# Second layer's self-attention: 32-row score groups, column-grouped values, an unrolled loop

## What is computed

```python
cq = _layernorm(x @ W_dq, q_ln_g, q_ln_b)          # 256 -> 64
Q = cq @ W_uq                                      # 64 -> 256
ckv = _layernorm(x @ W_dkv, kv_ln_g, kv_ln_b)
KV = ckv @ W_ukv
K, V = (KV[..., :D], KV[..., D:])
q, k, v = (t.reshape(B, S, N_HEADS, DH) for t in (Q, K, V))
scores = jnp.einsum('bqhd,bkhd->bhqk', q, k) / math.sqrt(float(DH))
scores = scores * jnp.tril(jnp.ones((S, S)))
scores = jnp.where(scores == 0, -jnp.inf, scores)  # also where a product is exactly 0
attn = jax.nn.softmax(scores, axis=-1)
out = jnp.einsum('bhqk,bkhd->bqhd', attn, v).reshape(B, S, D)
return out @ W_o.T
```

## Time and profile before

| | us |
|---|---|
| median of 3 runs (lowest to highest) | 4347.18 (4345.33 to 4351.53) |
| the profiled execution, its own time | 4351.41 |
| its span, first to last instruction | 4349.6 |
| its mean granted TensorE clock | 0.885 of full speed |

### The profile page before, as it was taken

One profiled execution on the slowest core, in us unless ns is written; L12 is line 12 of the kernel. 1 busy time (PEld: TensorE's weight loads), 2 busy tenths in 40 slices (PEclk: granted clock), 3 DMA queues, 4 the chain that ended last, 5 costly groups with the idle time before them and its releaser, 6 DMA issues. The chain is left out here.

```text
span 4349.6 us, 51903 instructions
## 1 busy us (share of the span) xinstructions
PE 3389.6 (78%) x16452; PEld 2208.8 (51%) x16453; DVE 2264.0 (52%) x5392; ACT 1485.2 (34%) x4021; POOL 864.8 (20%) x829
## 2 busy tenths in 40 slices
PE   6585994747989889856697688897888868876994
PEld 3553672325767667633374365344563345654663
DVE  6545553436666656457863466315642365743223
ACT  3212661213544545333102244213432124531331
POOL 2103012041010010110151545004520030030113
PEclk9776997868999999978798899898999889987997
DMA  1000001010000000000000000000000000013112
GB/s 55 1 1 11 1 1 63 5 46 1 1 2 2 1 2 1 19 30 10 0 1 13 26 1 1 27 0 26 1 6 22 15 11 7 1 50 142 33 34 69
DMA packets 34663, 80.29 MB, mean 18 GB/s; under 512 B 8433, under 2 KB 23554, under 8 KB 30306
## 3 DMA queue, kind: packets, MB, share of 16 engines
q1 hardware_dynamic: 28594, 63.03, 4.0%
q0 software_dynamic: 4368, 11.93, 1.0%
q10 hardware_dynamic: 1440, 2.12, 0.1%
HBM read 63.04 MB, written 14.02 MB: 18 GB/s over the span
## 5 line engine op out<-in xcount | busy, mean ns | idle before, releaser
L2159 PE MATMUL psum<-KT,Q_heads 128*128 x768 | 298.8, 500 | 23.0 <-DVE Q_heads L2199 23.0
L2171 PE MATMUL psum<-probsT,V_heads 128*128 128x128 f32 x2304 | 304.0, 278 | 0.0
L2220 DVE TENSOR_SCALAR zero_marks<-psum 128x128 f32<-128x128 f32 (+7 forms) x256 | 193.8, 757 | 199.7 <-PE psum L2162 199.6
L2171 PEld LDWEIGHTS psum<-probsT,V_heads 128*128 128x128 f32 x2304 | 284.3, 195 | 0.0
L2242 ACT ACTIVATE scores<-scores,max 128x128 f32<-128x128 f32 (+7 forms) x256 | 198.1, 774 | 158.4 <-DVE max L2224 157.2
L2254 ACT ACTIVATE probsT<-psum 128x128 f32<-128x128 f32 (+7 forms) x256 | 166.5, 650 | 214.1 <-PE psum L2186 214.1
L213 POOL TENSOR_SCALAR Xtok<-Xtok,ln_stats 128x256 f32<-128x256 f32 x144 | 174.2, 1217 | 295.2 <-DVE ln_stats L192 295.2
L2186 PE MATMUL psum<-ident,scores 128*128 128x128 f32 x1152 | 181.2, 284 | 62.9 <-ACT scores L2242 61.1
L2222 DVE CUSTOM_DVE_ANT_0 scores<-psum,zero_marks 128x128 f32<-128x128 f32 (+7 forms) x256 | 194.1, 758 | 30.6 <-issue 1.9
L2145 POOL TENSOR_TENSOR V_heads<-V,head_cols 128x1024 f32<-128x1024 f32 x32 | 81.8, 2590 | 594.5 <-PE psum L2171 527.6
L2186 PEld LDWEIGHTS psum<-ident,scores 128*128 128x128 f32 x1152 | 124.2, 142 | 140.7 <-ACT scores L2242 138.5
(11 more groups left out here) (606 smaller groups left out, 7360.5 us busy)
## 6 DMA issues: line engine op xcount, KB each, us to landing
W<-in_L3f_W SPq DMA_DIRECT2D x16, 1024.0 KB, 20.9
L3f_y_rows<-y SPq DMA_DIRECT2D x39, 128.0 KB, 1.7
L0f_rows<-Xtok SPq DMA_DIRECT2D x2, 2048.0 KB, 8.0
W<-in_L0f_W SPq DMA_DIRECT2D x3, 1152.0 KB
Wqkv<-in_L2f_Wqkv SPq DMA_DIRECT2D x2, 1536.0 KB, 8.5
W<-in_L2f_W SPq DMA_DIRECT2D x2, 1536.0 KB
XT<-in_xT SPq DMA_DIRECT2D x1, 2048.0 KB, 7.9
Xtok<-in_xtok SPq DMA_DIRECT2D x1, 2048.0 KB, 13.1
```

What stands on the lines that cost most here:

```text
L2159: pe.matmul(sc(i)[:, o:e], Qh[:, q % 2, h, :], KT[:, bass.ds(u * S + o, e - o)], start=True, stop=(e < n), skip_group_check=True)
L2171: ins = pe.matmul(ob(q)[:, 0:P], Vh[:, kt, h, :], PT[:, i % 2, kt * P:(kt + 1) * P], start=(h == 0 and kt == 0), stop=(h == HPC - 1 and kt ...
L2220: dve.tensor_scalar(zero[:, 0:n], sc(i)[:, 0:n], 0.0, NEG, ALU.is_equal, ALU.mult)
```

## The change

- The zeros that separate heads move. An array row group of 32 holds two heads. The projections write two copies of the queries, `Q[:, par]`, each with the heads of the other parity zeroed and with -1/4 already multiplied in (`sign`). A score product then uses only the 32 rows of its pair of heads. `Q_heads` and its DVE work are gone; since the scores are negated, the kernel takes a minimum, with `scale=-1.0` in the exponential, and the scaling of the maximum (L2224) is gone.
- For blocks 5 to 8 the keys from 512 on are projected into the partitions turned by 64, and `Qt` holds the queries turned likewise, so the two halves of one step's keys lie in two different row groups and in two PSUM banks.
- The values: V is kept in two copies by parity, and a product has 32 stationary columns, that pair's, and writes 32 output partitions. Heads are taken in the order 0, 2, 4, 6, 1, 3, 5, 7, and the values of four steps (a quad, four different column groups) are issued together after every fourth `turn`. `V_heads` and its POOL work are gone; POOL spreads the reciprocals instead of DVE.
- The loop is written out, 256 steps in one sequence. The score buffer in SBUF has 3 slots (2 before), probsT 6 (2 before). PE's order is turn(i), score(i+2), and after each fourth step the quad. ACT's order is exponential(i+1), then copy(i), the other way round than before.
- Projections are one phase (`L1_attn_projections`) with 4 more query jobs of 512 columns and wider weights; a small phase makes `masked` and `sign`. The output is written to the other activation buffer, the keys to the present one.

The diff, cut to its core:

```diff
+HALF_TURN = P // 2
+HEAD_ORDER = (0, 2, 4, 6, 1, 3, 5, 7)
+QUAD = 4
+def L1_attn_projections(nc, K, cT, uq, ukv, sign, Q, Qt, KT, V):
+    for c in range(DC):
+        for j in range(NB):
+            cols = slice(j * BLK, (j + 1) * BLK)
+            jobs.append(("Q", uq[:, c * P:(c + 1) * P], c_block(j), [Q[:, par, c, cols] for par in range(2)]))
+            if j % 2 == 1:
+                jobs.append(("Q", uq[:, D + c * P:D + (c + 1) * P], c_block(j), [Qt[:, par, c, j // 2, :] for par in range(2)]))
+            k0 = 2 * D if j % 2 == 1 else 0
+            jobs.append(("K", ukv[:, k0 + c * P:k0 + (c + 1) * P], c_block(j), [KT[:, c, cols]]))
+    for t in range(NT):
+        jobs.append(("V", cT[:, t * P:(t + 1) * P], ukv[:, D:2 * D], [V[:, par, :, t, :] for par in range(2)]))
...
+            ROT, SLOTS = 3, 6
...
                 @block.tensor
+                    def score(i):
+                        g, par, n = h // 2, h % 2, keys_of(i)
+                        here = slice(32 * g, 32 * g + 32)
+                        there = slice(32 * ((g + 2) % 4), 32 * ((g + 2) % 4) + 32)
+                        if i >= 2:
+                            pe.wait_ge(s["min_done"], i - 1)
+                        first = min(n, BLK)
+                        pe.matmul(sc(i)[:, 0:first], Q[here, par, c, t0:t0 + P], KT[here, c, b * S:b * S + first],
+                                  start=True, stop=(n > BLK), skip_group_check=True)
+                        if n > BLK:
+                            pe.matmul(sc(i)[:, BLK:n], Qt[there, par, c, b, (q - TPB) * P:(q - TPB + 1) * P], KT[there, c, b * S + BLK:b * S + n],
+                                      start=True, stop=False, skip_group_check=True)
+                        pe.matmul(sc(i)[:, n - P:n], K.identb[:], masked[:], start=False, stop=True, skip_group_check=True).then_inc(s["scored"], 1)
+                    def turn(i):
+                        pe.wait_ge(s["exp_done"], i + 1)
+                        if i >= 1:
+                            pe.wait_ge(s["pt_out"], i)
+                        for kt in range(keys_of(i) // P):
+                            ins = pe.transpose(turned[:, kt * P:(kt + 1) * P], Sc[:, i % ROT, kt * P:(kt + 1) * P], K.ident[:])
+                    def values(quad):
+                        pe.wait_ge(s["pt_out"], i0 + QUAD)
+                        for kt in range(q + 1):
+                            for i in range(i0, i0 + QUAD):
+                                g = slice(32 * (h // 2), 32 * (h // 2) + 32)
+                                ins = pe.matmul(ob(u)[g, 0:P], V[:, h % 2, c, b * QT_ + kt, g], PT[:, i % SLOTS, kt * P:(kt + 1) * P],
+                                                start=(first and kt == 0), stop=(last and kt == q), skip_group_check=True)
+                    for i in range(N):
+                        turn(i)
+                        if i + 2 < N:
+                            score(i + 2)
+                        if i % QUAD == 0 and i > 0:
+                            values(i // QUAD - 1)
...
                 @block.vector
+                        dve.wait_ge(s["scored"], i + 1)
+                        if i >= ROT:
+                            dve.wait_ge(s["turned"], i - ROT + 1)
+                        if i >= 2:
+                            dve.wait_ge(s["min_done"], i - 1)
+                        dve.tensor_scalar(zero[:, i % 2, 0:n], sc(i)[:, 0:n], 0.0, -NEG, ALU.is_equal, ALU.mult)
+                        dve.drain()
+                        dve.tensor_tensor_reduce(Sc[:, i % ROT, 0:n], sc(i)[:, 0:n], zero[:, i % 2, 0:n], 1.0, -NEG, ALU.add, ALU.min,
+                                                 low[:, i % ROT:i % ROT + 1]).then_inc(s["min_done"], 1)
...
                 @block.scalar
+                        if i + 1 < N:
+                            exp(i + 1)
+                        act.wait_ge(s["turned"], i + 1)
+                        if i >= SLOTS:
+                            act.wait_ge(s["pv_done"], (i - SLOTS) // QUAD + 1)
+                        act.activation(PT[:, i % SLOTS, 0:n], turned[:, 0:n], ACT.Copy).then_inc(s["pt_out"], 1)
```

More of the change, by code:

```diff
@@ L2092, in L1_attn @@
                 arrive(nc, K)
[L2093 to L2104, removed]
+                with phase(nc, K.sems, "step") as (block, s):
@@ L2120, in L1_attn @@
             Rx, RT = (sbuf(inside, nc, n, [P, 2, P]) for n in ("recip_spread", "recipT"))
[L2121 to L2125 removed]
+            units = [(c, b, q) for c in range(DC) for b in range(B) for q in range(QT_)]
+            steps = [(u, h) for u in range(len(units)) for h in HEAD_ORDER]
+            N, U = len(steps), len(units)
+            keys_of = lambda i: (units[steps[i][0]][2] + 1) * P
@@ L2126, in L1_attn @@
+            names = "scored min_done exp_done turned pt_out pv_done recip_done r_spread r_turned rt_out out"
             with phase(nc, K.sems, names) as (block, s):
                 sc = lambda i: K.psum[:, 2 * (i % 2):2 * (i % 2) + 2, :].rearrange("p b k -> p (b k)")
[L2128 to L2138, removed]
+                turned = K.psum[:, 4:6, :].rearrange("p b k -> p (b k)")
+                ob = lambda u: K.bank[6 + u % 2]
@@ L2148, in _ @@
                 @block.tensor
                 def _(pe):
[L2150 to L2184, removed]
-                            for kt in range(i // HPC + 1):
-                                ins = pe.transpose(K.bank[4 + kt // 4][:, (kt % 4) * P:(kt % 4 + 1) * P], Sc[:, i % 2, kt * P:(kt + 1) * P], K.ident[:])
-                            ins.then_inc(s["turned"], 1)
-                            if i > 0:
-                                values(i - 1)
-                        values(N - 1)
-                        turn_over(pe, u, (s["max_done"], N), (s["out"], QT_))
@@ L2261, in L1_attn, with exp @@
-        OTv = OT[:].rearrange("p (c t) -> p c t", c=DC)
-        finish(nc, K, lambda k, t: Wo[:, k, :], tile_of_block(OTv), DC)
+                    def exp(i):
+                        u, h = steps[i]
+                        act.wait_ge(s["min_done"], i + 1)
+                        if i % HPC == 0 and u >= 2:
+                            act.wait_ge(s["recip_done"], u - 1)
+                        p = Sc[:, i % ROT, 0:keys_of(i)]
+                        act.activation(p, p, ACT.Exp, bias=low[:, i % ROT:i % ROT + 1], scale=-1.0, accum_out=sums[:, u % 2, h:h + 1]).then_inc(s["exp_done"], 1)
```

193 lines of the change are left out of this document (114 added, 79 removed).

## The result

| | before | after |
|---|---|---|
| median, us | 4346.5 | 4431.06 |
| lowest to highest of 4 runs | 4345.33 to 4351.53 | 4424.08 to 4437.39 |
| ratio to before, 95% interval | | 1.0192 [1.0173, 1.0210] |
| profiled execution, its own time, us | 4351.41 | 4433.8 |
| its span, us | 4349.6 | 4432.1 |

A forecast was written before the change was run, and what follows sets the result against it. The chain over DVE, ACT and PE sets the pace: steps 650 us, with waits and edges 669, plus 57 for the clock, 726 against 786; projections net +3, so 4294, median 4290 us, range 4222 to 4395.

The forecast's parts named there:

- The clock: Attention phase: TensorE falls to 1.2 GHz in each block 1 and returns in the course of block 3; 57 us.
- clock does not come back in time: Rival, chance 0.19: 1.2 GHz lasts past block 3; 4341 after block 4, 4387 after block 5, 4546 if never.
- a wait and the edges: Attention phase: 10 us for one more wait ahead of DVE's pair, 3 for the first step, 6 for last values and output.
- though partly by changes of shape: Clock term: at 1.2 GHz PE is occupied without a hole from block 3 on, partly by changes of shape.
- The rule that two steps take PE's part and the chain: Attention steps: score(i+2) follows turn(i), so two steps take U + M; 3.64 us a step in block 8.
- U: PE's own part between two turns: 0.108 r + 0.215 min(r, 4) + 0.06 + 0.40, 2.18 us for r = 8.
- M: The chain over DVE, exponential and ACT's copy: 1.27 + 0.48 r, 5.11 us for r = 8 as path.
- The key halves: Scores of blocks 5 to 8: two row groups stream side by side, 0.86 us in place of up to 1.72.
- PE waits for ACT's copy: Sign in the profile: block 8 steps near 3.65 us with PE waiting for ACT's copy, not DVE.
- POOL's copy of the reciprocals: PE's turn of the reciprocals waits for POOL's spreading copy; stall bounded by 0 and 0.5 us a block, taken as 0.
- A quad of 64 pairs in block 8: Values of four steps in four column groups: 0.03 us a pair, V = 0.24 r + 0.4 a quad.
- The round trip: Change of PE's shape and back, once every step and once more every quad: 0 to 0.45 us, taken as 0.40.

The follow-up runs named there:

- e3_fill32: The changed kernel plus one unread product of 32 rows and 256 columns after every score(i+2); 4629.51 us.
- e11_serial: The changed kernel, but both key halves of blocks 5 to 8 use the same 32 rows, so they follow each other; 4525.71 us.
- e10_shape: e4_fullrow plus a product of 32 rows and 8 columns between turn(i) and score(i+2), so every step changes shape and back; 4345.91 us.
- e4_fullrow: The changed kernel with scores from all 128 rows again, queries spread by GpSimd, keys unturned, turned query jobs gone; 4230.59 us.
- e1_act_swap: The changed kernel with only ScalarE's order changed back to copy(i), then exponential(i+1); 4358.16 us.

## Why the prediction was wrong

**The step that failed** is "The clock": "I choose the return in the course of block 3", and with it the silent assumption that from there the clock stays at 2.4 GHz. It did not come back for good in any pass. By blocks, the four passes' steps against those predicted: blocks 1 and 2 together 4 us over (the fall was foreseen), block 3 6 over, block 4 36 over, blocks 5 to 8 112 over. That is 158. Beside the steps the sum held 19 for a wait and the edges, and outside the steps the phase spent 7, 12 less. That makes 146; the miss, from 726 to 871, is 145. The rival "clock does not come back in time" was there with 0.19, and its price list ran from 4341 to 4546. The result lies in it, but between its points: it knew "up" and "down", while the kernel alternated.

**Why the reading misled.** The earlier trace rows showed a return after 3.4 us in which PE was busy throughout. I took "occupied without a hole" for the condition. The rows of e3_fill32 (27.70 of 27.70 busy, clock 0.50) and of the changed kernel's 88.8 us from 1021.20 show that it is not. All work in the earlier trace rows used 128 rows; the 32-row scores take 382 of the 788 us that PE is busy in the new phase. The sentence "though partly by changes of shape" named half of it, and the 32-row scores, which e11_serial beside e10_shape shows to be what kept the clock down from block 3 on, were not weighed.

**What was right.** At 1.2 GHz the steps of blocks 2 and 3 were given as 2.34 and 3.06 and measured 2.29 and 3.00. The rule that two steps take PE's part and the chain held at 2.4 GHz: with 128-row scores (U = 0.323 r + 0.06, no change of shape) the same M gives 0.40 r + 0.67, for blocks 4 to 8 2.27, 2.67, 3.07, 3.48 and 3.88, measured 2.35, 2.76, 3.16, 3.60 and 3.89. The key halves run side by side. PE waits for ACT's copy. POOL's copy of the reciprocals takes 0.29 us and PE did not wait for it. A quad of 64 pairs in block 8 takes 1.89 us at 2.4 GHz (e4_fullrow, 1334.69 to 1336.58), where 2.3 was said; so four column groups do give the quarter, 0.030 us a pair. The round trip, taken at 0.40, is 0.26 in the changed kernel and 0.49 with the small product of e10_shape. The projections and the rest moved by less than 3 us. By the 81 ns a pair of the Trainium skill, page "TensorE: Matmul & The Clock Gate", section "Back-to-back issue gap", such a quad would be 5.2 us, an estimate; the row says 1.89.

```profile
1334.69 1.95 PE L2246 MATMUL psum<-probsT,V 128*32 128x128 f32 x64
1336.58 1.09 PE L2231 MATMUL psum<-ident,scores 128*128 128x128 f32 x8
```

**How the number divides.** The same order of work with the clock up is e4_fullrow, 200 us below the changed kernel though its key halves follow each other. What the change removes is real: at 4231 the unrolled loop, the values in column groups and the spreading moved off DVE are 2.8% better than before. The 32-row scores took that away and 1.9% more.

**Open.** Why the clock alternates just so in blocks 5 to 8 is not known; with ScalarE's order changed back (e1_act_swap) it stays up longer there. In blocks 1 and 2 the share of the rows and that of the changes of shape were not separated: e10_shape shows that the second suffices there, and no kernel had 32-row scores without changes of shape.

## What to carry to other kernels

Before packing small products into row groups, ask what TensorE's clock will do with the work that remains: PE showing busy 100% at 0.50 is a worse bound than PE waiting at 1.00, and here the wasteful 128-row score (seven eighths of its rows multiply zeros) was 200 us faster. Read the granted clock block by block, and test it by adding 128-row work that nobody needs: if the kernel gets faster, the clock was the bound.

## What the runs showed that I had not expected

- TensorE stayed at 1.2 GHz for 88.8 us while busy 87.33 of them, and in e3_fill32 through a whole block with PE busy 27.70 of 27.70 us.
- 254 added products of 128 rows, 109 us of work at full clock, made the kernel 87 us faster; the same with 32 rows made it 198 us slower.
- With the same number of changes of shape, 32-row scores ran block 5 of the second pass at 0.50 throughout (e11_serial) and 128-row scores at 1.00 (e10_shape).
- Four column groups of 32 stationary columns take 0.030 us a pair of load and product over 128 moving columns, and two row groups of 32 rows stream at the same time, started 6 to 8 ns apart.
- A swap of two ScalarE instructions was worth 73 us where it let the clock stay up in some blocks, and 38 us where the clock was up anyway.
